# Layer 0: `v` of three groups in four by a 1x1 product and nine taps, two of them on ScalarE; two sums on GpSimd; a new order on all engines

## The chip, the cores and the metric

The kernel runs on one core of one Trainium2 chip. The metric is the device time of one execution in microseconds; the time before is the median of three runs. TensorE is called PE in the rows, VectorE DVE, ScalarE ACT and GpSimd POOL.

## The reference

Two layers, each added to its input, on four images of 64 channels and 256 x 256 pixels. Only layer 0 is touched by the change.

```python
# layer 0, x normalized by _gn first
hidden = jnp.einsum('bchw,oc->bohw', x, w_hidden) + b_hidden[None, :, None, None]
hidden = jax.lax.conv_general_dilated(hidden, w_dw[:, None, :, :], window_strides=(1, 1), padding='SAME', feature_group_count=hid, ...) + b_dw[None, :, None, None]
q, k, v = jnp.split(hidden, 3, axis=1)
out = jnp.fft.irfft2(rfft2(patches(q)) * rfft2(patches(k)), s=(8, 8))      # by 8x8 patch
out = (out - mu) / jnp.sqrt(var + 1e-05) * ln_w + ln_b                     # over the 128 channels
y = x + jnp.einsum('bchw,oc->bohw', v * out, w_proj) + b_proj
```

## The kernel before

Layer 0 works on strips of 8 image rows (128 strips in all, 32 per image) and cuts each strip into 4 groups of 64 columns, so 512 groups. A loop iteration does two strips; a "half" below is one strip, four groups, and the groups of a half are called j to j+3. Every engine has its own queue, written out by hand as a function `body`, and the engines meet at semaphores only. An engine works strictly in its order, so a wait at the head of a queue holds all that stands behind it.

What happens to a strip first: ScalarE normalizes it into `xn` (`normed`, L782, two halves), VectorE multiplies its edge rows (`masks`, L901), ScalarE rounds it to 16 bits (`high_parts`, L788), GpSimd makes the rests (`low_parts`, L573, two halves), and VectorE copies high and low parts into the stacks that TensorE reads: `high_below` (L921), `high_stacks` (two products at L910, four copies at L914 to L917) and `both_stacks` (three copies at L927). TensorE may begin a strip only when its stacks are there.

What happens to a group: `q` and `k` come out of TensorE as four tiles of 14 matmuls (`conv`, L625). ScalarE copies them (L795), TensorE makes the transform (`forward`, L697), ScalarE copies its parts (`k_swap`, `q_im`, `q_re`, L818 to L823), VectorE and GpSimd multiply and add them (`product`, L936 on VectorE; `imaginary` with its two steps L583 and L586 on GpSimd; the mean by `means`, L965 and L967, on VectorE and `less_mean`, L592, on GpSimd), and TensorE transforms back (`inverse`, L688).

`v` is made in two ways, by turns. In every second group TensorE does all of it: 14 matmuls of 512 columns (`conv_v`, L644), and ScalarE copies the result (`v_copy`, L803). In the others TensorE makes a small 1x1 product with the hidden weights (`hidden`, L660 to L664) into PSUM, and the 3x3 filter is done by taps: ScalarE does the middle one (`middle_tap`, L810), VectorE the other eight, each a multiply-add into `v_s` (`taps`, L959).

At the end of a pair of groups come `times_v` (L947, VectorE), `variance` (L714), `project` (L674 and L676), the root on ScalarE (L835, L837), and on VectorE `finish` (L982 makes `t_n`, L983 adds bias and residual) and `output` (L993 adds `t_n`, L995 takes the statistics). In part of the iterations VectorE also takes statistics of the following images (`x_chunk`, L1002).

## Time and profile before

| | us |
|---|---|
| median of three runs | 8745.06 (8741.76 to 8749.92) |
| profiled execution, its own time | 8754.59 |
| its span | 8752.8 |
| layer 0, from about 140 to 6196 us of the span | 6056 |
| busy in the whole span: TensorE, VectorE, ScalarE, GpSimd | 96%, 85%, 72%, 55% |

The granted clock of TensorE is 0.993 of its full speed as a mean over the span. The busy shares are means over both layers; what a change in layer 0 does must be read from the stretch of layer 0, and there from the order in which the four queues meet.

### The profile page before, as it was taken

The page shows a single profiled execution, that of the slowest core. Times are in us where ns is not written, and L with a number is a line of the kernel's source. Part 1 is how long each engine was busy: PE and PEld are TensorE (multiplying, and loading weights), DVE is VectorE, ACT ScalarE, POOL GpSimd, SP SyncE. Part 2 cuts the span into 40 slices and gives each one's busy share as a digit, 9 for nine tenths or more (in the row PEclk, how much of TensorE's full clock was granted, in tenths as well). Part 3 has the DMA queues.
Part 4 walks back from the last instruction along what each step waited for, and adds up shares of the span by engine and source line. Part 5 has one row for each costly group of instructions (what it writes and reads, how often), then busy time and mean ns, then how long its engine had stood idle before and what let it go on. Part 6 is the DMA issues. An engine that isn't in the chain of part 4 may idle for free. (4 is left out here: it accounts for less than half of the span.)

```text
span 8752.8 us, 169999 instructions
## 1 busy us (share of the span) xinstructions
PE 8435.8 (96%) x57716; PEld 4818.6 (55%) x57716; DVE 7480.2 (85%) x9839; ACT 6324.6 (72%) x8629; POOL 4840.4 (55%) x2723
## 2 busy tenths in 40 slices
PE   2999999999999999999999999999879999999999
PEld 1666666666666666666666666666323333333333
DVE  6888888888888888888888888888759999999998
ACT  2777777777777777777777777777208888888887
POOL 1444444444444444444444444444109999999998
PEclk9999999999999999999999999999999999999999
DMA  6222222222222222222222212212694555555554
GB/s 154 54 68 61 55 68 63 55 67 54 64 68 53 64 56 66 64 56 65 64 49 55 54 43 54 54 43 54 146 203 114 119 119 119 119 119 119 119 119 111
DMA packets 613650, 711.27 MB, mean 81 GB/s; under 512 B 44029, under 2 KB 572507, under 8 KB 589575
## 3 DMA queue, kind: packets, MB, share of 16 engines
q1 hardware_dynamic: 611022, 690.44, 33.9%
q10 hardware_dynamic: 2488, 18.98, 1.0%
q8 instruction: 87, 1.43, 0.1%
q14 instruction: 53, 0.43, 0.0%
HBM read 548.96 MB, written 164.11 MB: 81 GB/s over the span
## 5 line engine op out<-in xcount | busy, mean ns | idle before, releaser
L625 PE MATMUL banks<-w_hi,hi_lo 128*128 128x256 f16 x18432 | 2362.6, 273 | 35.1 <-DVE hi_lo L927 35.1
L625 PEld LDWEIGHTS banks<-w_hi,hi_lo 128*128 128x128 f16 x18432 | 1737.7, 98 | 844.9 <-issue 533.5
L583 POOL TENSOR_TENSOR u_im<-q_im,k_swap 128x512 f32<-128x512 f32 x512 | 741.3, 1448 | 1810.4 <-ACT q_im L821 1723.8
L959 DVE SCALAR_TENSOR_TENSOR v_s<-banks,tap_w,v_s 128x512 f32<-128x512 f32 x2048 | 1535.1, 750 | 55.0 <-ACT v_s L810 0.6
L1511 PE MATMUL banks<-z,conv_w 128*128 128x512 f32 x3096 | 1556.0, 618 | 1.2 <-ACT z L1639 1.2
L1482 POOL TENSOR_TENSOR part_sum<-part_sum,prod 128x1024 f32<-128x1024 f32 x645 | 1525.2, 2365 | 52.2
L795 ACT ACTIVATE qk<-banks,inv_wscale 128x512 f32<-128x512 f32 x1024 | 706.5, 690 | 910.2 <-PE banks L625 903.7
L586 POOL TENSOR_TENSOR u<-u,u_im 128x512 f32<-128x512 f32 x512 | 725.3, 1417 | 766.8 <-DVE u L936 766.8
L625 PE MATMUL banks<-w_lo_pair,hi_pair 128*128 128x256 f16 x6144 | 1006.1, 273 | 0.0
L592 POOL TENSOR_TENSOR u<-u,u_mean 128x512 f32<-128x512 f32 x512 | 532.2, 1040 | 733.7 <-DVE u_mean L967 733.7
L1511 PEld LDWEIGHTS banks<-z,conv_w 128*128 128x128 f32 x3096 | 521.5, 188 | 628.1 <-issue 570.5
L936 DVE TENSOR_TENSOR u<-q_re,banks 128x512 f32<-128x512 f32 x512 | 350.6, 685 | 529.9 <-ACT q_re L823 526.4
L573 POOL TENSOR_TENSOR hl_all<-xn,hi_all 64x1280 f16<-64x1280 f32 x258 | 702.1, 2721 | 137.8 <-ACT hi_all L788 100.9
L782 ACT ACTIVATE xn<-xr,par 128x1408 f32<-128x1408 f32 x258 | 746.9, 2895 | 16.7 <-DMA xr<-in_x_dram 9.8
L688 PEld LDWEIGHTS banks<-idft,u 128*128 128x128 f32 x4096 | 498.1, 192 | 261.4 <-issue 168.9
L625 PEld LDWEIGHTS banks<-w_lo_pair,hi_pair 128*128 128x128 f16 x6144 | 601.5, 98 | 69.9
L688 PE MATMUL banks<-idft,u 128*128 128x128 f32 x4096 | 568.5, 282 | 33.6 <-POOL u L592 25.0
L644 PE MATMUL banks<-hi_lo,w_hi 128*128 128x512 f16 x2304 | 544.2, 382 | 22.0 <-DVE tmp L1028 22.0
L625 PE MATMUL banks<-w_lo_one,hi_side 128*128 128x256 f16 x2048 | 558.5, 273 | 0.0
L625 PE MATMUL banks<-w_lo_one,hi_ind 128*128 128x256 f16 x2048 | 558.4, 273 | 0.0
L697 PE MATMUL banks<-qk,dft 64*32 64x512 f32 x8192 | 557.6, 601 | 0.0
L1788 DVE TENSOR_TENSOR prod<-banks,x_up 128x1024 f32<-128x1024 f32 x387 | 471.0, 1221 | 58.1 <-PE banks L1493 52.1
(252 smaller groups left out, 15777.1 us busy)
## 6 DMA issues: line engine op xcount, KB each, us to landing
xr<-in_x_dram SPq DMA_DIRECT2D x258, 640.0 KB, 9.1
xb<-y_scratch SPq DMA_DIRECT2D x262, 320.0 KB, 4.7
xa<-y_scratch SPq DMA_DIRECT2D x262, 256.0 KB, 5.4
x_res<-in_x_dram SPq DMA_DIRECT2D x258, 256.0 KB, 4.1
out_dram<-res SPq DMA_DIRECT2D x258, 256.0 KB, 3.3
y_scratch<-ys SPq DMA_DIRECT2D x256, 256.0 KB, 3.9
prod<-y_scratch SPq DMA_DIRECT2D x256, 256.0 KB, 5.6
xs<-in_x_dram SPq DMA_DIRECT2D x92, 512.0 KB, 7.4
```

What stands on the lines that cost most here:

```text
L573: nc.gpsimd.tensor_tensor(hl_all[C:P, 1 + c0:1 + c1, 1:SL], xn[C:P, c0:c1, 0:SL - 1], hi_all[C:P, 1 + c0:1 + c1, 0:SL - 1], ALU.subtract). ...
L583: nc.gpsimd.tensor_tensor(u_im[:], q_im[:], k_swap[:], ALU.mult).then_inc(u_made, 1)
L586: nc.gpsimd.tensor_tensor(u[:], u[:], u_im[:], ALU.add).then_inc(u_step, 1)
L625: r = pe.matmul(out, px, w, start=n == 0, stop=n == 13)
L644: r = pe.matmul(b_v[:], w, px, start=n == 0, stop=n == 13)
L688: last = pe.matmul(by_patch[:, p, t], u[:, block], idft[:], start=True, stop=True)
L697: last = pe.matmul(b_f[p][fr, :], dft[px, part, :], qk[px, 2 * half:2 * half + 2, :], start=True, stop=True)
L782: act.activation(xn[:, cols, 0:SL], xr[b][:, :, cols].rearrange("p s w -> p w s"), ACT.Identity, bias=par[b][:, 1:2], scale=par[b][:, 0:1] ...
L795: act.activation(qk[:, 2 * h:2 * h + 2, :], b_qk[h][:].rearrange("p (t c) -> p t c", t=2), ACT.Copy, scale=inv_wscale[:, 0:1]).then_inc(qk ...
L959: v.scalar_tensor_tensor(v_out, hidden_v[:, 1 + dc:GCOL + 1 + dc, 1 + dr:R + 1 + dr], tap_w[:, t:t + 1], v_out, ALU.mult, ALU.add).then_in ...
L1482: nc.gpsimd.tensor_tensor(part_sum[:], prod[0][:] if n == 0 else part_sum[:], prod[n + 1][:], ALU.add)\
L1511: last = pe.matmul(b_c[h][:], conv_w[:, n, :], z[b][:, 2 * h + j:2 * h + j + 2, dc:dc + W], start=n == 0, stop=n == 5)
```

## The change

It makes `v` by `conv_v` only in the first group of each strip; the three others take the 1x1 product and taps. ScalarE now does two of the nine taps: the middle one as before (`first_tap`), and the one at the lower right (`side_tap`), which it writes to a buffer of its own, `side`. VectorE does the seven left. GpSimd adds `side` to `v_s` (`side_sum`), and it takes over the sum of `t_n` into the output (`output_sum`), which VectorE did in `output`. The bodies of all engines are written in a new order, and groups are numbered so that a body reaches back into the strips before and ahead into the next; the old `tail` functions give way to bodies before the first and behind the last iteration. `k_swap`, `q_im` and `q_re` are separate steps. The sizes of all other operations stay. The core of the diff, without the functions that only take other indices:

```diff
@@ -420,6 +421,10 @@
...
+                def side_sum(i, j):
+                    if real(i, j):
+                        pool.wait_ge(v_tapped, tapped(i, j) * 7)
+                        pool.wait_ge(v_side, tapped(i, j))
+                        nc.gpsimd.tensor_tensor(v_s[j % 4][:], v_s[j % 4][:], side[:], ALU.add).then_inc(v_summed, 1)
+                def output_sum(i, jp):
+                    if real_pair(i, jp):
+                        out = ys[jp // 2 % 2][:, :, GCOL * (jp % 2):GCOL * (jp % 2) + GCOL]
+                        pool.wait_ge(fin_read, i * 4 + (jp + 1))
+                        pool.wait_ge(t_made, i * 4 + (jp + 1))
+                        nc.gpsimd.tensor_tensor(out, out, t_n[:].rearrange("p (c r) -> p r c", r=R), ALU.add).then_inc(fin_step, 1)
...
+                    for h in range(2):
+                        j, jp, js = 4 * h, 2 * h, h
+                        imaginary(i, j)
+                        if real(i, j):
+                            pool.wait_ge(u_made, i * 8 + (j + 1))
+                        low_parts(i, js + 1, 0)
+                        complex_sum(i, j)
+                        side_sum(i, j + 1)
+                        if real(i, j + 1):
+                            pool.wait_ge(v_summed, tapped(i, j + 1))
+                        low_parts(i, js + 1, 1)
+                        less_mean(i, j)
+                        imaginary(i, j + 1)
+                        complex_sum(i, j + 1)
+                        less_mean(i, j + 1)
+                        imaginary(i, j + 2)
+                        side_sum(i, j + 2)
+                        output_sum(i, jp - 1)
+                        complex_sum(i, j + 2)
+                        less_mean(i, j + 2)
+                        imaginary(i, j + 3)
+                        complex_sum(i, j + 3)
+                        side_sum(i, j + 3)
+                        less_mean(i, j + 3)
+                        output_sum(i, jp)
...
+                            pe.wait_ge(tops_ready, i * 2 + (j // 4 + 1))
+                            pe.wait_ge(stacks_ready, i * 2 + (j // 4 + 1))
...
+                    if real(i, j):
+                        if j % 4 == 1:
+                            pe.wait_ge(v_copied, i * 2 + (j // 4 + 1))
+                        else:
+                            pe.wait_ge(v_tapped, (tapped(i, j) - 1) * 7)
+                            pe.wait_ge(v_side, tapped(i, j) - 1)
+                        need(pe, t_made, i * 4 + (projected + 1))
...
+                    for h in range(2):
+                        j, jp, js = 4 * h, 2 * h, h
+                        tile(i, j, 1)
+                        tile(i, j, 2)
+                        tile(i, j, 3)
+                        inverse(i, j - 2)
+                        project(i, jp - 2, j - 1, then_forward=j)
+                        forward(i, j)
+                        value(i, j, image if h == 0 else None)
+                        inverse(i, j - 1)
+                        hidden(i, j + 1, jp - 2)
+                        tile(i, j + 1, 0)
+                        tile(i, j + 1, 1)
+                        tile(i, j + 1, 2)
+                        tile(i, j + 1, 3)
+                        variance(i, jp - 1, then_forward=j + 1)
+                        forward(i, j + 1)
+                        project(i, jp - 1, j + 1)
+                        tile(i, j + 2, 0)
+                        hidden(i, j + 2, jp - 1)
+                        tile(i, j + 2, 1)
+                        tile(i, j + 2, 2)
+                        inverse(i, j)
+                        tile(i, j + 2, 3)
+                        tile(i, j + 3, 0, then_forward=j + 2)
+                        forward(i, j + 2)
+                        tile(i, j + 3, 1)
+                        tile(i, j + 3, 2)
+                        inverse(i, j + 1)
+                        tile(i, j + 3, 3)
+                        hidden(i, j + 3, jp - 1)
+                        variance(i, jp)
+                        tile(i, j + 4, 0, then_forward=j + 3)
+                        forward(i, j + 3)
...
+                def side_tap(i, j):
+                    if real(i, j):
+                        act.wait_ge(v_hidden, tapped(i, j))
+                        need(act, v_summed, tapped(i, j) - 1)
+                        act.activation(by_column(side[:]), hidden_v[:, 2:GCOL + 2, 2:R + 2], ACT.Copy, scale=tap_w[:, 8:9])\
+                            .then_inc(v_side, 1)
...
+                        exp_root(i, jp - 2)
+                        key_swap(i, j)
+                        v_copy(i, j)
+                        query_imaginary(i, j)
+                        first_tap(i, j + 1)
+                        side_tap(i, j + 1)
+                        square(i, j - 1)
+                        high_parts(i, js + 1)
...
-                                               v_out, ALU.mult, ALU.add).then_inc(v_tapped, 1)
-
...
+                            if n == 0:
+                                v.wait_ge(v_begun, tapped(i, j))
+                                v.wait_ge(v_side, tapped(i, j))
...
+                        both_stacks(i, js)
+                        times_v(i, j - 3)
+                        product(i, j - 2)
+                        taps(i, j - 1, 0, 1)
+                        params(i, js + 2)
+                        taps(i, j - 1, 1, 3)
+                        sums(i, j - 2)
+                        taps(i, j - 1, 3, 4)
+                        means(i, j - 2)
+                        taps(i, j - 1, 4, 7)
+                        product(i, j - 1)
+                        if h == 0 and not first and (stats or image == NI - 1):
+                            x_chunk(i)
...
+                        sums(i, j - 1)
...
+                        shifted(i, jp - 2)
+                        means(i, j - 1)
+                        times_v(i, j - 2)
+                        masks(i, js + 1)
...
+                        scaled(i, jp - 2)
+                        output(i, jp - 3)
+                        product(i, j)
+                        output(i, jp - 2)
+                        taps(i, j + 1, 0, 4)
+                        times_v(i, j - 1)
+                        taps(i, j + 1, 4, 7)
+                        high_below(i, js + 1)
+                        sums(i, j)
+                        means(i, j)
+                        scaled(i, jp - 1)
+                        high_stacks(i, js + 1)
+                        taps(i, j + 2, 0, 1)
+                        product(i, j + 1)
+                        taps(i, j + 2, 1, 3)
+                        sums(i, j + 1)
+                        taps(i, j + 2, 3, 4)
+                        means(i, j + 1)
+                        taps(i, j + 2, 4, 5)
+                        times_v(i, j)
+                        taps(i, j + 2, 5, 6)
+                        shifted(i, jp - 1)
+                        taps(i, j + 2, 6, 7)
 
```

On VectorE, in an ordinary iteration, the row of stack copies at the end of a strip's preparation, before: the `high_stacks` rows, `params`, then `both_stacks` follow one another directly.

```order
L910 TENSOR_SCALAR hi_ind1<-ind,par1 64x256 x2
L914 COPY hi_pair1<-hi_all 128x2064
L915 COPY hi_ind1<-hi_all 64x2064
L916 COPY hi_side1<-hi_all 64x2064
L917 COPY hi_side1<-hi_all 64x2048
L893 COPY par0<-tab0 128x6
L927 COPY hi_lo1_0<-hl_all 128x2064
L927 COPY hi_lo1_1<-hl_all 128x2064
L927 COPY hi_lo1_2<-hl_all 128x2064
L936 TENSOR_TENSOR u<-q_re,banks1 128x512
L947 TENSOR_TENSOR w_v1<-banks3,v_s1 128x512
```

The same place now: the `both_stacks` copies (L1085) stand at the end of the half, directly behind the last tap (L1122) of group j+2.

```order
L1122 SCALAR_TENSOR_TENSOR v_s2<-banks2,tap_w,v_s2 128x512
L1135 TENSOR_SCALAR u_mean<-u_mean 128x4
L1122 SCALAR_TENSOR_TENSOR v_s2<-banks2,tap_w,v_s2 128x512
L1106 TENSOR_TENSOR w_v0<-banks3,v_s0 128x512
L1122 SCALAR_TENSOR_TENSOR v_s2<-banks2,tap_w,v_s2 128x512
L1153 SCALAR_TENSOR_TENSOR ys1<-banks3,b_proj,x_res1 128x8x64
L1122 SCALAR_TENSOR_TENSOR v_s2<-banks2,tap_w,v_s2 128x512
L1085 COPY hi_lo1_0<-hl_all 128x2064
L1085 COPY hi_lo1_1<-hl_all 128x2064
L1085 COPY hi_lo1_2<-hl_all 128x2064
```

So the copies moved behind seven taps, a product and the sums of a later group.

On GpSimd, the end of an ordinary half before: between two `less_mean` rows (L592) there is only the pair of L583 and L586.

```order
L573 TENSOR_TENSOR hl_all<-xn,hi_all 64x128x10
L583 TENSOR_TENSOR u_im<-q_im,k_swap 128x512
L586 TENSOR_TENSOR u<-u,u_im 128x512
L592 TENSOR_TENSOR u<-u,u_mean 128x512
L583 TENSOR_TENSOR u_im<-q_im,k_swap 128x512
```

And now, from the second `low_parts` row (L600) of a half on:

```order
L600 TENSOR_TENSOR hl_all<-xn,hi_all 64x128x10
L625 TENSOR_TENSOR u<-u,u_mean 128x512
L611 TENSOR_TENSOR u_im<-q_im,k_swap 128x512
L618 TENSOR_TENSOR u<-u,u_im 128x512
L625 TENSOR_TENSOR u<-u,u_mean 128x512
L611 TENSOR_TENSOR u_im<-q_im,k_swap 128x512
L633 TENSOR_TENSOR v_s2<-v_s2,side 128x512
L641 TENSOR_TENSOR ys1<-ys1,t_n 128x8x64
L618 TENSOR_TENSOR u<-u,u_im 128x512
```

The rows L633 (`side_sum`, waits for the last tap of j+2) and L641 (`output_sum`) are new on this queue and stand between L611 and L618 of group j+2.

## Rows read from the trace of the kernel before

**Rows 1.** Stretches, layer 0: start:end length, busy (x) PE, PEld, DVE, ACT, POOL, clock, DMA, GB/s.
```profile
140.00:6196.00 6056.00, 5979.95 (x50171) 4013.79 (x50172) 5122.06 (x7279) 4494.30 (x6021) 2700.99 (x1794) 1.00 0.25 59
```

**Rows 2.** One line's instructions, `v_copy`: count, shortest/median/longest ns, first to last start.
```profile
L803 ACT ACTIVATE v_s<-banks,inv_wscale x64: 662/687/694, 4605.7 to 6079.8; 128x512 f32<-128x512 f32 x64
```

**Rows 3.** Waits of TensorE, 300 to 6160 us: us in total, times, longest.
```profile
PE banks L688 <- POOL u L592: 19.4, 63, 1.6
```

**Rows 4.** Timeline of TensorE: start us, us, engine, line, operation, operands, count.
```profile
5046.65 2.11 PE L644 MATMUL banks<-hi_lo,w_hi 128*128 128x512 f16 x9
...
5049.77 1.09 PE L697 MATMUL banks<-qk,dft 64*32 64x512 f32 x16
5050.79 1.16 PE L625 MATMUL banks<-w_hi,hi_lo 128*128 128x256 f16 x9
...
5052.33 1.06 PE L688 MATMUL banks<-idft,u 128*128 128x128 f32 x8
5053.22 1.15 PE L625 MATMUL banks<-w_hi,hi_lo 128*128 128x256 f16 x9
...
5054.75 0.28 PE L660 MATMUL banks<-hi_lo,hid_hi 128*128 128x264 f16 x1
...
5055.55 1.16 PE L625 MATMUL banks<-w_hi,hi_lo 128*128 128x256 f16 x9
...
5066.82 1.08 PE L674 MATMUL banks<-v_s,proj_shift 128*64 128x512 f32 x4
...
5068.69 1.16 PE L625 MATMUL banks<-w_hi,hi_lo 128*128 128x256 f16 x9
```

**Rows 5.** One line's instructions, `both_stacks`, over the steady stretch (columns as in rows 2).
```profile
L927 DVE COPY hi_lo<-hl_all x372: 689/824/833, 339.3 to 6133.9; 128x2064 f16<-128x2064 f16 x186
```

**Rows 6.** Timeline of VectorE (columns as in rows 4).
```profile
5043.61 0.95 DVE L921 COPY hl_all<-hi_all 64x2816 f16<-64x2816 f16 x1
...
5047.91 3.81 DVE L910 TENSOR_SCALAR hi_ind<-ind,par 64x256 f16<-64x256 f16 x2
...
5053.22 0.82 DVE L916 COPY hi_side<-hi_all 64x2064 f16<-64x2064 f16 x1
5054.05 1.67 DVE L917 COPY hi_side<-hi_all 64x2048 f16<-64x2048 f16 x1
...
5055.81 2.17 DVE L927 COPY hi_lo<-hl_all 128x2064 f16<-128x2064 f16 x3
5057.90 0.68 DVE L936 TENSOR_TENSOR u<-q_re,banks 128x512 f32<-128x512 f32 x1
...
5061.35 4.68 DVE L959 SCALAR_TENSOR_TENSOR v_s<-banks,tap_w,v_s 128x512 f32<-128x512 f32 x6
5065.95 1.08 DVE L993 TENSOR_TENSOR ys<-ys,t_n 128x512 f32<-128x512 f32 x1
```

**Rows 7.** Timeline of GpSimd (columns as in rows 4).
```profile
5043.84 1.85 POOL L586 TENSOR_TENSOR u<-u,u_im 128x512 f32<-128x512 f32 x1 [0.77 <-DVE u L936]
5046.70 1.04 POOL L592 TENSOR_TENSOR u<-u,u_mean 128x512 f32<-128x512 f32 x1 [1.00 <-DVE u_mean L967]
5047.81 2.71 POOL L573 TENSOR_TENSOR hl_all<-xn,hi_all 64x1280 f16<-64x1280 f32 x1
5053.50 1.67 POOL L583 TENSOR_TENSOR u_im<-q_im,k_swap 128x512 f32<-128x512 f32 x1 [2.97 <-ACT q_im L821]
5058.73 1.28 POOL L586 TENSOR_TENSOR u<-u,u_im 128x512 f32<-128x512 f32 x1 [3.56 <-DVE u L936]
```

**Rows 8.** Timeline of ScalarE (columns as in rows 4).
```profile
5050.96 0.58 ACT L818 COPY k_swap<-banks 64x512 f32<-64x512 f32 x1 [0.40 <-PE banks L697]
...
5052.74 0.68 ACT L821 ACTIVATE q_im<-banks,imag_sign 64x512 f32<-64x512 f32 x1
...
5056.01 0.78 ACT L810 ACTIVATE v_s<-banks,tap_w 128x512 f32<-128x512 f32 x1
```

**Rows 9.** Timeline of VectorE where the next images' statistics are made.
```profile
3035.61 2.46 DVE L1002 BATCH_NORM_STATS2 x_stats<-xs 128x6 f32<-128x512 f32 x4
```

710 lines of the change are left out of this document (355 added, 355 removed).

## The prediction

> **What bounds the kernel now.** I read the stretches first: in layer 0 TensorE is busy 5980 of 6056 us, VectorE 5122, ScalarE 4494, GpSimd 2701 [rows 1]. Then the pace: 63 intervals of two groups between 4605.7 and 6079.8, 23.40 us each, so a half (one strip) takes 46.8 us [rows 2]; the halves with statistics keep this pace too. Then the waits of TensorE: only 19.4 us in 63 waits, for the mean-free product [rows 3]. So TensorE bounds layer 0 by its own work, and VectorE, with 5122 of 6056, has some 7 us of a half to spare. The last view is the timeline of all engines side by side, where VectorE and GpSimd turn out to be less independent than the busy times say.
>
> **TensorE's part.** One of the two `conv_v` of a half becomes a `hidden`. Start to start, `conv_v` takes 5049.77 - 5046.65 = 3.12 us and `hidden` 5055.55 - 5054.75 = 0.80 [rows 4]. That frees 2.32 us per half, and with 128 halves 297 us. If TensorE still bounded, the pace would be 44.5 us and the kernel 8745 - 297 = 8448.
>
> **VectorE's part.** Taps: 3 x 7 instead of 2 x 8, five more. Six taps behind one another take 4.68 with 0.75 for the last, so 0.79 from tap to tap, and the next other instruction starts 0.67 behind the last tap's start, an overlap of 0.08 [rows 6]; with it `product` and `times_v` (0.68) count 0.60. Five more taps are 3.8 us. Two sums L993 of 1.08 leave, 2.2. Net +1.6 per half: busy time alone would still fit into 44.5. On ScalarE three `side_tap` of about 0.78 and one `first_tap` for one `v_copy` of 0.69 come in [rows 8, 2], +2.4, into some 12 us of slack per half: free as long as its order keeps pace. GpSimd gets 3 `side_sum` and 2 `output_sum`.
>
> **How VectorE and GpSimd get in each other's way.** At 5047.81 GpSimd starts the 2.71 us of `low_parts`; VectorE starts its two products of `high_stacks` at 5047.91 and is through with both only at 5051.72, 1.20 after GpSimd's end at 5050.52 [rows 6, 7]. Later the copy L916 is running (5053.22 to 5054.04) when GpSimd starts L583 at 5053.50: GpSimd needs 1.67, ending 1.13 after the copy, and the next copy L917, 0.69 by itself (1.67 with 0.98 of standing), ends 0.55 after GpSimd. So these copies and GpSimd's instructions take turns, one whole instruction each, while taps (PSUM and one buffer) show no such spread. The Trainium skill, SBUF — State Buffer, section Who interferes with whom, says the same, that whoever issues first holds the shared port pair for the whole instruction and the other fully blocks; were it a mere slowing of both, the terms below would be smaller. The three copies of `both_stacks`, 2.17 us together, never met GpSimd before: their longest is 833 ns in 372 [rows 5], as GpSimd stands idle there (5055.17 to 5058.73).
>
> Now both new GpSimd instructions meet them. `side_sum` of j+2 waits for the last tap of j+2, and the instruction behind this tap on VectorE is the first copy of `both_stacks`; `output_sum` stands directly behind `side_sum`. So copy, sum (1.13), copy, sum (1.13), copy: 2.17 becomes 4.4. Behind these copies waits TensorE, which opens the next strip with a tile that needs `stacks_ready`. What `output_sum` takes on GpSimd no row shows. Bounds: 1.04 (L592, in place) and 2.71 (L573) [rows 7]; I take 1.27 as for the sums of the same size. The Trainium skill, GPSIMD Engine Reference, section Engine selection, speaks against the move: elementwise work on two inputs runs about 2x slower there than on VectorE, by which 1.08 becomes an estimated 2.2 us.
>
> **The cycle that this makes**, worked along one half. Time zero: `side_tap` of j+1 is written and VectorE starts the taps of j+1.
> - Seven taps with a `times_v` between: 3 x 0.79 + 0.67 + 0.60 + 2 x 0.79 + 0.67 = 5.9.
> - `high_below` 0.95, then a wait: the complex sum of j on GpSimd may only follow `low_parts`, and is held by `high_below` to 1.13 behind it (as 5043.84 + 1.85 against 5043.61 + 0.95), so 1.2 more. 8.0.
> - `sums`, `means`, `scaled`: 1.4. 9.4.
> - `high_stacks`. GpSimd's second `low_parts`, released by the last tap of j+1, has just started: 2.7 standing, 1.2 for the two products, `less_mean` of j between them 0.9, 3.0 for the four copies, `imaginary` of j+1 between them 0.98. 8.8 (before, without `less_mean` between: 5055.72 - 5047.91 = 7.8 [rows 6]). 18.2.
> - Seven taps of j+2, six of them followed by something else, 6 x 0.67 + 0.79 = 4.8; between them `product` 0.60, `times_v` 0.60, `shifted` 0.8 (a multiply-add like a tap), `sums` and `means` 0.8. 7.6. 25.8.
> - `both_stacks` 4.4. 30.2.
> - TensorE from the tile of the new strip to the end of `forward` j: four tiles at 1.54 = 6.2, two `forward` at 1.02, `inverse` 0.89, `project` 1.87 [rows 4]: 11.0. 41.2.
> - ScalarE then, in its order: `query_real`, `exp_root`, `key_swap`, `v_copy`, `query_imaginary`, `first_tap`, `side_tap`. Two copies at about 1.1 each, 0.6, 0.69, 1.4, 0.7, 0.7 [rows 8]: 6.6, in which TensorE makes `conv_v`, `inverse` and `hidden` beside it. 47.8, and the taps of the next strip start.
>
> So the cycle is 47.8 us against 46.8. TensorE, with 44.5 of work, then waits at three places: at `forward` j+2 for `product` j+1 (1.6), at `inverse` j+1, and above all at the first tile of a strip (2 us). Its granted clock was 1.00 through layer 0 [rows 1]; I leave it there, though waits of this length are new.
>
> In the halves with `x_chunk`, 2.46 us [rows 9], the order is `product`, `x_chunk`, `sums`, `shifted`, `means`, `times_v`, `masks`, `scaled`, and `hidden` j+1 waits for `scaled`; about 1.6 of the 2.46 lie in time that VectorE has there, 0.85 come through to the cycle, in some 46 halves: 39 us.
>
> Image changes (three), filling and draining I take as unchanged: the same chains, in other places. I take the transfers as hidden as before; the load of a strip is now asked for later, behind a later `output`, and if it came late `normed` on ScalarE would wait for it. The sum against the profiled execution: 8754.6 + 128 x 1.0 + 39 = 8922; it stood 9.5 above the median, so 8910.
>
> **The rivals.**
> 1. The copies of `both_stacks` are not met, or the sums slip behind them. The cycle is then 47.8 - 2.2 = 45.6: 8745 - 128 x 1.2 + 39 = 8630. For it: 2.2 us hang on two instructions arriving within a microsecond. Against it: both are released by the tap that stands just before the copies. 0.22.
> 2. TensorE bounds on. Both collisions would have to cost under a microsecond together: 8448, between 8400 and 8550. For it: VectorE's part of this cycle would be 23.4 us without any standing, not 30.2. Against it: 3.6 us of standing per half (2.6 and 0.98) are in the rows of before already. 0.13.
> 3. Slower still: `output_sum` takes 2.2 us. Then `both_stacks` ends 0.9 later, and `output` in front of the taps of j+1, which waits for the other `output_sum`, passes 0.4 on. 1.3 x 128 = 166: 9075. It decides from about 1.7 us on. 0.10.
> 4. Gain and loss cancel within 0.2% (17 us, about what a measurement of this kernel can tell from no change): 0.06.
>
> **How the numbers follow.** My forecast, 8910 with 8800 to 9000 of its own, gets 0.49. It is above 8762 throughout, as is rival 3: slower 0.59. Rivals 1 and 2: faster 0.34, as a sliver of rival 1 falls into no change: 0.07 with rival 4. The range takes in rival 1 and most of rival 3, and leaves out rival 2: 8590 to 9080.
>
> **What would show it.** In the new profile the copies of `both_stacks` should have a median near 1.6 us or a longest near 1.8 where it was 833 ns, `side_sum` near 1.9 to 2.0, TensorE should wait some 2 us at each strip's first tile for L1085, and two `v_copy` (now one per half) should stand 47.8 us apart. If the copies are still at 0.8, rival 1 holds; if TensorE hardly waits and the pace is 44.5, rival 2; if `output_sum` is above 2 us, rival 3. I would be wrong altogether if the hold between the two engines were weaker for 16-bit copies next to float sums than L917 shows.

## The result and the profile after

| | time, us | ratio to before, 95% interval |
|---|---|---|
| before | 8747.5 (4 runs) | |
| after | 9282.6 (9274.1 to 9285.3, 4 runs) | 1.061 (1.0591 to 1.0628) |
| predicted | 8910 (8590 to 9080) | 1.019 |

The changed kernel is 6.1% slower. Its profiled execution has a span of 9283.5 us and a mean granted clock of 0.969 (before: 8752.8 and 0.993). The direction was forecast, the size was not: the profiled execution took 9285.3 us, 363 more than the sum of 8922 that was made for it, and the median lies outside the range. Of the 531 us between the two spans 525 lie in the 127 halves of layer 0 (6505.6 us from the first `v_copy` of layer 0 to that of its last strip, against 5980.5 before); filling and draining are as long as they were, to 5 us.

The page and the stretches of the four long loops of layer 0 (columns as in [rows 1]); TensorE is no longer busy throughout, and its clock, 1.00 in [rows 1], is 0.96 to 0.97:

```profile
PE 8473.3 (91%) x57204; PEld 4892.6 (53%) x57204; DVE 7966.9 (86%) x10207; ACT 6569.2 (71%) x9010; POOL 5826.4 (63%) x3361
...
320.00:1490.00 1170.00, 1072.75 (x8831) 727.24 (x8830) 1001.98 (x1361) 840.59 (x1135) 658.07 (x432) 0.96 0.25 58
1600.00:3060.00 1460.00, 1335.54 (x10985) 905.72 (x10983) 1251.59 (x1718) 1051.81 (x1419) 816.77 (x539) 0.96 0.24 57
3160.00:4640.00 1480.00, 1355.67 (x11192) 921.47 (x11191) 1274.40 (x1741) 1066.18 (x1441) 832.38 (x547) 0.96 0.25 58
4750.00:6200.00 1450.00, 1337.38 (x11104) 910.91 (x11102) 1236.56 (x1680) 1058.73 (x1430) 820.58 (x543) 0.97 0.21 49
```

The waits of the changed kernel, 300 to 6600 us (us in total, times, longest). [rows 3] had 19.4 us in all for TensorE's wait on the mean-free product. Three kinds are new: TensorE for `both_stacks` (L1085), TensorE for nothing that the profile shows ("issue"), and VectorE for TensorE's `inverse` (L794). The remaining row, VectorE for the complex sum, has grown from 107 us:

```profile
DVE u L1095 <- PE banks L794: 439.4, 123, 7.2
DVE u_mean L1129 <- POOL u L618: 255.7, 200, 1.5
PE banks L681 <- DVE hi_lo L1085: 231.0, 109, 2.2
PE banks L681 <- issue: 166.6, 78, 3.5
```

The copies of `both_stacks`, which answer to [rows 5] (ns, shortest/median/longest), and the two new kinds of sums on GpSimd, `output_sum` (L641) and `side_sum` (L633):

```profile
L1085 DVE COPY hi_lo<-hl_all x345: 820/1772/2152, 300.3 to 6153.2; 128x2064 f16<-128x2064 f16 x173
L641 POOL TENSOR_TENSOR ys<-ys,t_n x256: 1515/1535/1979, 221.8 to 6733.4; 128x512 f32<-128x512 f32 x128
L633 POOL TENSOR_TENSOR v_s<-v_s,side x384: 1259/1280/1991, 185.4 to 6720.0; 128x512 f32<-128x512 f32 x192
```

**How long a half is.** The starts of two `v_copy`, one per half now, stand apart by different amounts. Between 5100 and 5303 us they are 48.4, 54.4, 48.4 and 51.9 us. Over the kernel the 46 halves with an `x_chunk` in them have a mean of 52.6 and the 81 others of 50.4. The shortest in the loops, 48.4, is near the 47.8 of the prediction; the others are not. (The difference of 2.2 us is not the price of `x_chunk`: it stands in the same half of an iteration as the turn of TensorE's loop, which is read below.)

One such short half on VectorE, from the first taps of j+1 to the same point in the next half:

```profile
5103.17 3.11 DVE L1122 SCALAR_TENSOR_TENSOR v_s<-banks,tap_w,v_s 128x512 f32<-128x512 f32 x4
...
5109.03 0.96 DVE L1074 COPY hl_all<-hi_all 64x2816 f16<-64x2816 f16 x1
5111.15 0.69 DVE L1129 TENSOR_REDUCE u_mean<-u 128x4 f32<-128x512 f32 x1 [1.17 <-POOL u L618]
...
5113.50 3.64 DVE L1061 TENSOR_SCALAR hi_ind<-ind,par 64x256 f16<-64x256 f16 x2
...
5118.65 1.89 DVE L1067 COPY hi_side<-hi_all 64x2064 f16<-64x2064 f16 x1
...
5121.28 0.75 DVE L1122 SCALAR_TENSOR_TENSOR v_s<-banks,tap_w,v_s 128x512 f32<-128x512 f32 x1
...
5128.71 4.58 DVE L1085 COPY hi_lo<-hl_all 128x2064 f16<-128x2064 f16 x3
5133.21 0.68 DVE L1106 TENSOR_TENSOR w_v<-banks,v_s 128x512 f32<-128x512 f32 x1
...
5151.54 1.54 DVE L1122 SCALAR_TENSOR_TENSOR v_s<-banks,tap_w,v_s 128x512 f32<-128x512 f32 x2
```

From taps to the end of the stacks this is 30.0 us (5103.17 to 5133.21), and to the next taps 18.3 more.

And TensorE's first tile of a strip, in a short half (first three rows), in the one of 51.9 us (the next four) and in the one of 54.4 us (the last two, the second and third tile of the strip):

```profile
5133.53 1.15 PE L681 MATMUL banks<-w_hi,hi_lo 128*128 128x256 f16 x9 [2.12 <-DVE hi_lo L1085]
...
5135.16 1.09 PE L815 MATMUL banks<-qk,dft 64*32 64x512 f32 x16
5136.18 1.16 PE L681 MATMUL banks<-w_hi,hi_lo 128*128 128x256 f16 x9
...
5284.65 1.19 PE L681 MATMUL banks<-w_hi,hi_lo 128*128 128x256 f16 x9 [2.12 <-DVE hi_lo L1085]
5285.64 0.84 PE L681 MATMUL banks<-w_lo_pair,hi_pair 128*128 128x256 f16 x3
...
5286.84 1.96 PE L815 MATMUL banks<-qk,dft 64*32 64x512 f32 x16
5290.80 1.14 PE L681 MATMUL banks<-w_hi,hi_lo 128*128 128x256 f16 x9 [2.01 <-issue]
...
5187.80 2.08 PE L681 MATMUL banks<-w_hi,hi_lo 128*128 128x256 f16 x9 [2.07 <-issue]
...
5190.74 2.13 PE L681 MATMUL banks<-w_hi,hi_lo 128*128 128x256 f16 x9
```

The reader is to see three things here that the first three rows don't have. In the 51.9 us half the three matmuls on `hi_pair` take 0.84 us (0.49 in a short half) and the forward transform 1.96 instead of 1.09: behind the wait the array runs at the lower of its two levels (1.2 instead of 2.4 GHz; the granted clock is 0.50 from 5285.7 to 5288.7, and 1.00 at the same place of the short half, behind a wait of the same 2.12 us). Before the second tile of the strip TensorE idles 2.01 us with no releaser. That tile is the first work of the loop's body: it is where TensorE's loop turns back. And in the 54.4 us half the clock is at 0.50 behind this turn too, from 5187.8 to 5193.4, so that nine matmuls take 2.08 and 2.13 us instead of 1.15. That is the difference between 51.9 and 54.4.

### The profile page after: what moved, and what is told of

It reads as the page before. It is cut to its first block and busy times, and to the rows that moved or that the text cites. A ratio compares the mean times of both kernels' runs of the same rounds, so it can differ in the third digit from the quotient of the medians.

```text
span 9283.5 us, 176870 instructions
## 1 busy us (share of the span) xinstructions
PE 8473.3 (91%) x57204; PEld 4892.6 (53%) x57204; DVE 7966.9 (86%) x10207; ACT 6569.2 (71%) x9010; POOL 5826.4 (63%) x3361
## 5 line engine op out<-in xcount | busy, mean ns | idle before, releaser
L681 PE MATMUL banks<-w_hi,hi_lo 128*128 128x256 f16 x18432 | 2443.9, 279 | 427.1 <-DVE hi_lo L1085 269.4
L681 PEld LDWEIGHTS banks<-w_hi,hi_lo 128*128 128x128 f16 x18432 | 1795.3, 100 | 1127.8 <-issue 900.0
L1122 DVE SCALAR_TENSOR_TENSOR v_s<-banks,tap_w,v_s 128x512 f32<-128x512 f32 x2688 | 2009.2, 747 | 58.6 <-ACT side L927 7.1
L1647 POOL TENSOR_TENSOR part_sum<-part_sum,prod 128x1024 f32<-128x1024 f32 x645 | 1525.1, 2365 | 52.5 <-POOL part_sum L1647 0.4
L618 POOL TENSOR_TENSOR u<-u,u_im 128x512 f32<-128x512 f32 x512 | 745.8, 1457 | 707.9 <-DVE u L1095 697.8
L611 POOL TENSOR_TENSOR u_im<-q_im,k_swap 128x512 f32<-128x512 f32 x512 | 694.9, 1357 | 739.3 <-ACT k_swap L936 405.8
L600 POOL TENSOR_TENSOR hl_all<-xn,hi_all 64x1280 f16<-64x1280 f32 x256 | 695.4, 2716 | 485.1 <-ACT hi_all L897 424.0
L943 ACT ACTIVATE q_im<-banks,imag_sign 64x512 f32<-64x512 f32 x512 | 351.0, 685 | 582.2 <-PE banks L815 579.0
L641 POOL TENSOR_TENSOR ys<-ys,t_n 128x512 f32<-128x512 f32 x256 | 446.4, 1744 | 305.2 <-DVE t_n L1143 296.2
L633 POOL TENSOR_TENSOR v_s<-v_s,side 128x512 f32<-128x512 f32 x384 | 555.6, 1447 | 104.5 <-DVE v_s L1122 104.5
L815 PE MATMUL banks<-qk,dft 64*32 64x512 f32 x8192 | 603.0, 648 | 1.6 <-ACT qk L904 1.6
L919 ACT ACTIVATE v_s<-banks,tap_w 128x512 f32<-128x512 f32 x384 | 297.8, 775 | 408.3 <-PE banks L757 406.1
L1085 DVE COPY hi_lo<-hl_all 128x2064 f16<-128x2064 f16 x384 | 582.1, 1571 | 0.0
```

Source lines behind the costliest of these rows:

```text
L600: nc.gpsimd.tensor_tensor(hl_all[C:P, 1 + c0:1 + c1, 1:SL], xn[C:P, c0:c1, 0:SL - 1], hi_all[C:P, 1 + c0:1 + c1, 0:SL - 1], ALU.subtract). ...
L611: nc.gpsimd.tensor_tensor(u_im[:], q_im[:], k_swap[:], ALU.mult).then_inc(u_made, 1)
L618: nc.gpsimd.tensor_tensor(u[:], u[:], u_im[:], ALU.add).then_inc(u_step, 1)
L681: r = pe.matmul(out, px, w, start=n == 0, stop=n == 13)
L815: last = pe.matmul(b_f[p][fr, :], dft[px, part, :], qk[px, 2 * half:2 * half + 2, :], start=True, stop=True)
L1085: last = v.tensor_copy(hi_lo[b][d][:], hl_all[:, :, 1 + d:1 + d + R])
```

## The experiments

The runs ask, in this order: what the turn of TensorE's loop costs (e1), what the lower clock costs (e2, e16), why a turn costs at all (e8, e17, e18), what the two sums on GpSimd cost at `both_stacks` (e3 to e7), and which part of the change brings the loss (e9 to e15).

All ratios are to the kernel before, run beside it on the same chip. "Half" is the distance of two `v_copy` in the loops.

| kernel | us | ratio, 95% interval | halves, us |
|---|---|---|---|
| after | 9282.6 | 1.061 (1.059 to 1.063) | 48.4 to 54.4 |
| e1 turn elsewhere | 9040.3 | 1.034 (1.032 to 1.035) | 48.4, and 49.0 to 50.6 |
| e2 extra tile in the wait | 8995.1 | 1.029 (1.027 to 1.030) | 48.2, 48.8; one copy to 52.9 |
| e3 output sum later | 9035.4 | 1.033 (1.031 to 1.034) | 46.9 to 47.6, and 51.4 to 53.3 |
| e4 both sums narrow | 8854.3 | 1.013 (1.011 to 1.014) | 46.0 to 46.7, and 48.6 to 50.8 |
| e5 = e1, e2, e3 | 8930.5 | 1.020 (1.018 to 1.022) | 47.8, 48.3, some 49.5 to 51.5 |
| e6 stacks early, e1 | 8808.5 | 1.006 (1.004 to 1.008) | 47.2, 47.8 |
| e7 output sum on VectorE | 9159.3 | 1.047 (1.045 to 1.049) | 48.1, 48.9, and 51 to 54 |
| e8 before, turned as after | 8795.4 | 1.0045 (1.003 to 1.006) | |
| e9 side tap on VectorE | 8730.1 | 0.9976 (0.9966 to 0.9985) | 46.4, 47.2; in the first loop some of 52 to 53 |
| e10 both on VectorE | 8625.8 | 0.986 (0.984 to 0.988) | 45.5 to 46.4; in the first loop two of 49 and 52 |
| e11 = e10, e1 | 8614.3 | 0.985 (0.983 to 0.986) | 45.5 to 46.4 |
| e12 = e11, stacks early | 8799.2 | 1.0055 (1.004 to 1.007) | 47.0, 47.9 |
| e13 side sum later | 9292.8 | 1.062 (1.060 to 1.063) | 48.3 to 55.1 |
| e14 side sum on VectorE | 9197.8 | 1.051 (1.049 to 1.052) | 48.5, 49.3, and 51 to 54 |
| e15 = e13, e1 | 9099.9 | 1.040 (1.038 to 1.041) | 48.6, 50.2, 50.9 |
| e16 = e1, extra tile before the turn | 9032.9 | 1.032 (1.030 to 1.034) | 48.2 to 48.8, and 49.4 to 52.6 |
| e17 = e16, code shifted | 8989.4 | 1.027 (1.025 to 1.028) | 48.2 to 48.8, and 49.1 to 51.6 |
| e18 = e8, code shifted | 8756.1 | 1.0003 (0.999 to 1.001) | |

### e1: where TensorE's loop turns

The last tile and transform of a half's order become the first of the next:

```diff
                         j, jp, js = 4 * h, 2 * h, h
+                        tile(i, j, 0, then_forward=j - 1)
+                        forward(i, j - 1)
                         tile(i, j, 1)
...
                         variance(i, jp)
-                        tile(i, j + 4, 0, then_forward=j + 3)
-                        forward(i, j + 3)
```

> TensorE's loop body begins one tile earlier: the first tile of a strip and the forward transform behind it are written at the head of the next half instead of at the end of this one. The order of all instructions is the same, only the point at which TensorE's loop turns back moves from behind the forward transform to before the wait for the stacks. Theory of the loop's end (in the changed kernel TensorE sits idle 2.0 to 3.0 us before the second tile of every second strip, with no releaser, exactly where its loop turns back; a clean half takes 48.4 us, one with the loop's end 51.9): the turn now falls into the wait of about 2.1 us for both_stacks, so some 2 to 3.5 us come back every two halves: 64 x 2 to 3.5 = 130 to 220 us, 9060 to 9150 us. Rival, the idle time belongs to something else that stands there (the forward transform's result, the tile's buffer), or another chain is as late: 9270 to 9290 us and the same idle time at the same instruction.

Measured: 9040, 242 us less, a little more than the upper end of the expectation. No half above 50.6 us is left in the loops. The stretch 4750 to 6200 us had 37.1 us of idle time of TensorE without a releaser in the changed kernel, and has 10.0 here, all of it in the first 150 us, at the change of image; the wait for the stacks is as long as it was (after, then this run; columns as in the waits above):

```profile
PE banks L681 <- DVE hi_lo L1085: 50.8, 24, 2.1
PE banks L681 <- issue: 37.1, 19, 3.5
```

```profile
PE banks L681 <- DVE hi_lo L1085: 57.4, 27, 2.2
PE banks L681 <- issue: 10.0, 7, 2.0
```

So the turn of the loop costs the changed kernel 240 us, and the rival (something else stands there) is out, since not one instruction changed its place in the order. But the turn's own idle time is only about half of that: from 300 to 6200 us TensorE's idle time without a releaser goes from 155.0 to 38.7 us, by 116. The granted clock rises in the same run, from 0.96 to 0.97 in the four stretches of the changed kernel to 0.98 to 0.99. Behind 31 of the 47 turns of the changed kernel it stands at the lower level, as at 5187.8 us. The other half of the 240 us is, by this, the lower clock that the turn brings; no run parts the two.

### e2, e16: the clock

```diff
                         if j % 4 == 0 and t == 0:
+                            if not isinstance(i, int) or i * 8 + j > 0:
+                                pe.wait_ge(qk_copied, i * 16 + (2 * j - 1))
+                                conv((j // 4 + 1) % 2, b_qk[0][:, 0:KQ], 12, None)
                             pe.wait_ge(tops_ready, i * 2 + (j // 4 + 1))
```

> Before TensorE waits for the stacks of a new strip it computes one tile (14 matmuls, about 1.54 us) of the old strip into the bank that the first tile of the new one then overwrites: extra work without use, laid into a wait of 2.1 us. Theory of the clock (behind that wait the granted clock is at the lower of its two levels for some tiles, the forward transform behind it takes 1.96 us instead of 1.09 in many halves): the wait left is 0.6 us, the transforms are at 1.09, the mean granted clock of layer 0 goes from 0.965 towards 1.00, and 1 to 2 us come back in about half to all of the halves: 9280 - 100 to 200 = 9080 to 9180 us. Rival, the lower clock there has nothing to do with the wait: same clock, and the extra work costs nothing or makes it slower: 9280 to 9400 us.

Measured: 8995, 287 us less, more than either theory had: extra work makes the kernel faster. The granted clock is 0.99 to 1.00 in all four stretches. But not all of the gain is the clock. In three of the four loops the turn no longer costs anything either (halves of 48.2 and 48.8), and in the second, 1600 to 3060 us, it does (52.5). To part the two, e16 has the loop turning as in e1 and puts the extra tile ahead of the turn:

```diff
                         variance(i, jp)
+                        old_tile(i, j + 4)
```

(`old_tile` is the same two lines as above.)

> The changed kernel with TensorE's loop turning before the wait for the stacks, and one tile of extra work without use (the old strip's data into the bank that the new strip's first tile overwrites) at the end of the old strip, ahead of the turn. Against the run with the turn alone (9040 us, halves of 48.4 and 50.0 to 50.5 us by turns, the longer ones with a forward transform of 1.96 us behind the wait) it measures the clock alone. Theory of the clock: all halves at 48.2 to 48.8 us, the transforms at 1.09 us, 9040 - 63 x 1.9 = 8920 us, 8890 to 8960. Rival, the longer halves have another cause: 9020 us or more.

Measured: 9033, the same as e1 and in the range of the rival, but not for the rival's reason. The stretches of e16:

```profile
320.00:1490.00 1170.00, 1108.82 (x9447) 767.84 (x9445) 1036.71 (x1408) 869.74 (x1173) 678.22 (x446) 1.00 0.25 61
...
3160.00:4640.00 1480.00, 1431.97 (x12240) 993.88 (x12239) 1342.36 (x1825) 1127.54 (x1523) 879.81 (x580) 1.00 0.25 60
```

The clock is at 1.00, but the turn is back: in the first, second and fourth loop every second half is 49.5 to 52.6 us long, with up to 2.3 us of idle time at the turn. In the third the turn is free, and there the halves are 48.4 and 48.8 where e1 had 48.4 and 50.6. That is the clock alone: 49.5 - 48.6 = 0.9 us a half. In the fourth stretch e1 has a mean of 48.9, and runs without either cost 48.3 (e2, e17): 0.6. Over 128 halves the clock is 80 to 115 us, on top of what it takes behind the turn. As a check: 242 + 80 to 115, less the quarter or so of the turn's cost that stays in the second loop, is near the 287 of e2.

### e8, e17, e18: why a turn costs, and where

> The kernel before, with one edit: TensorE's loop turns back behind the first tile and the forward transform of the next strip, where the loop of the changed kernel turns, instead of before that tile. The order of all instructions is the same. It asks whether the turn costs time by its place alone. If the turn idles TensorE 2 to 3 us wherever nothing else covers it: 64 x 2 to 3 = 130 to 190 us slower, 8880 to 8940 us, with idle time before the inverse transform that follows. If it costs time only where TensorE has just waited and has nothing queued: within 10 us of the kernel before, 8745 to 8760 us.

The edit is that of e1 the other way round, in the kernel before:

```diff
+                    if not last:
+                        pe.wait_ge(stacks_ready, i * 2 + 3)
+                        pe.wait_ge(hi_made, i * 2 + 3)
+                        pe.wait_ge(qk_copied, i * 16 + 15)
+                        conv(0, b_qk[0][:, 0:KQ], 4 * ORDER[0], lambda: transform_ready(i, 7, True))
+                        forward()
```

(and the same lines skipped at the head of the body.) Measured: 8795, 41 us above the kernel before that ran beside it, between the two expectations. The profile says why: 32.8 us of idle time in 11 waits, all of them in the first of the four loops, none in the other three.

```profile
PE banks L688 <- issue: 32.8, 11, 3.3
```

The program holds a copy of the loop for each stretch between two images' statistics, and they run the same instructions. What differs is where the copy lies in TensorE's program. e17 and e18 move all copies by 70 matmuls:

```diff
+                        if isinstance(i, int) and i * 8 + j == 0 and t == 0:
+                            for extra in range(5):
+                                conv(0, b_qk[0][:, 0:KQ], 0, None)
```

> The run with the turn before the wait and the extra tile ahead of it, with 70 matmuls (five tiles without use, 7.7 us once) added in TensorE's program ahead of all its loops. Nothing else changes but the place of the loops' code. The program has four copies of the loop, one for each stretch between two images' statistics; without the shift the turn cost 2.3 us in the first, second and fourth copy and nothing in the third. If the cost of a turn hangs on where the copy of the loop lies in the program, other copies are hit now, and the time is between 8880 (none hit) and 9080 us (all four); if it hangs on the timing of the engines alone, the same copies are hit and the time is 9033 + 8 us.

> The kernel before with TensorE's loop turned behind the first tile and forward transform (8795 us; 11 waits of 3 us, all in the first of the four copies of the loop), with the same 70 matmuls ahead of all loops. If the place of the copy decides: the waits are in another copy, in more or in none, 8755 (none) to 8950 us; if it is only the timing (the first stretch is the one in which x_chunk starts): the first copy again, 8795 + 8 us.

Measured: e18 8756, the time of the kernel before (8753), no turn waited for in any copy. e17 8989, 44 us less than e16 though it has 7.7 us more to do, and other copies are hit. The idle time of TensorE without a releaser in e17, in the four stretches 320 to 1490, 1580 to 3080, 3160 to 4640 and 4750 to 6200 us:

```profile
PE banks L681 <- issue: 25.6, 23, 2.1
```
```profile
PE banks L681 <- issue: 9.9, 21, 1.2
```
```profile
PE banks L681 <- issue: 20.6, 28, 1.6
```
```profile
PE banks L681 <- issue: 8.6, 19, 1.0
```

In e16 these were 27.8, 34.7, 9.7 and 26.5 us: the third copy was free, now the second and the fourth are. (The 9 us that remain in a free copy are 0.35 us in each iteration between the extra tile and the stacks, and some 4 us at the change of image.) So the place of a loop's code decides whether its turn costs anything: in both kernels the shift is the only thing that lasts, and with it other copies pay, or none. That the work which TensorE still has queued decides how much of it shows fits e1 and e16, but no run tests it alone. The Trainium skill, Advanced Engine Details and Errata, section ISA Cache, gives a cache of instructions with lines of 16 KB, 256 instructions each. That a jump back can fall into a line which must be fetched again is my inference from it; no run here shows a line or a fetch. The changed kernel itself was not run with its code shifted, so how much of its 240 us is bad luck of place stays open.

### e3, e4, e7: the sums on GpSimd and both_stacks

```diff
                         side_sum(i, j + 2)
-                        output_sum(i, jp - 1)
                         complex_sum(i, j + 2)
                         less_mean(i, j + 2)
+                        output_sum(i, jp - 1)
```

> On GpSimd the first output sum of a half moves behind less_mean of j+2, so that of the two new GpSimd instructions only side_sum can meet the three both_stacks copies. Theory of the meeting (each 128x512 GpSimd sum holds the copies up by its own time of about 1.1 us): the three copies take 3.4 us instead of 4.57, TensorE waits 1.0 instead of 2.1 us for them, 1.1 us per half come back or somewhat more with the clock: 9280 - 140 = 9140, 9080 to 9180 us. Rival, the chain that ends last does not pass through both_stacks (another wait ends as late): 9260 to 9300 us although the copies are shorter.

Measured: 9035, 247 us less, beyond the expected range. One copy in three is still met (the first of the two rows below; the second is e4's), and the shortest half goes from 48.4 to 46.9, by 1.5 us. TensorE's wait for the stacks falls from 2.1 to 0.8 us. The turn costs more here, 4.5 to 6.4 us in every second half, and GpSimd's own loop shows one as well (205.0 us in 52 waits of up to 4.6 us before its first instruction, 300 to 6600 us).

```profile
L1085 DVE COPY hi_lo<-hl_all x358: 818/824/1784, 299.5 to 6179.2; 128x2064 f16<-128x2064 f16 x179
...
L1085 DVE COPY hi_lo<-hl_all x369: 820/825/1775, 339.6 to 6168.9; 128x2064 f16<-128x2064 f16 x185
```

e4 lets both sums work on 8 of 512 columns (`v_s[j % 4][:, 0:8]`, `out[:, 0:1, 0:8]`):

> Part of the computation is left out: side_sum and output_sum on GpSimd add only 8 of 512 columns; all waits and orders stay. It measures what the two new GpSimd instructions cost by their length. Theory of the meeting: the three both_stacks copies take 2.2 us instead of 4.57, TensorE hardly waits for them, the clock stays up, 2.4 to 4 us per half come back: 8780 to 8980 us. Rival, the cycle is set by the number of dependent steps on VectorE and by TensorE's loop, and not by the two sums: no more than 1 us per half, 9150 to 9280 us.

Measured: 8854, within the first theory. The shortest half is 46.0. One copy is still met, now by `imaginary`, so this isn't 2.2 but 3.2 us of stacks. The turn still idles TensorE 2.6 to 3.1 us, at places where it did not wait for the stacks at all.

e7 undoes one part of the change: `output_sum` on VectorE, behind `scaled` of one pair and behind `shifted` of the other.

```diff
+                        v.tensor_tensor(out, out, t_n[:].rearrange("p (c r) -> p r c", r=R), ALU.add).then_inc(fin_step, 1)
...
                         shifted(i, jp - 1)
+                        output_sum(i, jp - 1)
                         taps(i, j + 2, 6, 7)
```

> One part of the change undone: output_sum goes back from GpSimd to VectorE, behind scaled of the pair 2h-2 and behind shifted of the pair 2h-1. All else is as in the changed kernel. Theory of the meeting and of the cycle through VectorE: both_stacks is met by side_sum alone, 3.4 instead of 4.57 us, but the two sums of 1.08 us each stand on the same chain, one before the last tap of j+2 and one before the taps of j+1: 1 us per half slower in sum, 9283 + 0 to 250, 9400 us. Rival, the length of VectorE's order is not what ends last, and only the meeting counts: 1.1 us per half faster, 9140 us or less.

Measured: 9159, 123 us less, between the two and near the rival. On VectorE the sum takes 1.10 us (shortest 1.08), on GpSimd 1.52 at its shortest; the shortest half is 48.1.

### e5, e6, e12: edits put together

> The three earlier edits together: TensorE's loop turns before the wait for the stacks, one tile of extra work without use lies in that wait, and the first output sum on GpSimd stands behind less_mean of j+2. Theory (three separate causes: the loop's turn, the lower clock behind the wait, the meeting at both_stacks; each alone gave 240, 290 and 250 us, and the shortest halves in the runs were 48.4 us, and 46.9 with the output sum later): halves of 46.9 and, where x_chunk stands, 47.6: 127 x (50.9 - 47.2) = 470 us under the changed kernel, 8810 us, 8770 to 8860. Should the three give their gains in full one on top of the other: 9283 - 775 = 8510. Rival, GpSimd's own loop, which idled up to 4.6 us at its turn in the run with the output sum later, becomes the late one: above 8900.

e5 is e1, e2 and e3 in one. Measured: 8930, above its range and in the rival's. The extra tile now stands behind the turn and TensorE has less queued when it comes: in two of the four loops the turn costs 2 us again, and in the same two GpSimd's turn shows, up to 3.9 us. Gains of 242, 287 and 247 us alone, 776 in sum, came to 352 together.

In e6 `both_stacks` stands before the last tap, where no new sum can be released, and TensorE makes the new strip's first tile before `hidden`:

```diff
+                        tile(i, j, 0)
+                        hidden(i, j - 1, jp - 3)
+                        variance(i, jp - 2, then_forward=j - 1)
+                        forward(i, j - 1)
                         tile(i, j, 1)
...
-                        both_stacks(i, js)
...
                         shifted(i, jp - 1)
+                        both_stacks(i, js + 1)
                         taps(i, j + 2, 6, 7)
```

> TensorE's loop turns before the wait for the stacks, as in the first experiment. On VectorE both_stacks stands before the last tap of j+2 instead of behind it, so that side_sum and output_sum, which wait for that tap or stand behind one that does, can't meet it. On TensorE the first tile of the new strip stands before hidden and variance instead of behind them, since these wait for the last tap. Theory of the meeting: the three copies take 2.2 us instead of 4.57, TensorE doesn't wait for them, forward j+3 starts some 2 us earlier and the clock stays up: halves of 46.0 to 46.9, 8650 to 8800 us. Rival, hidden of j+3 now waits for the last tap, which ends only 0.7 us sooner than both_stacks did without the meeting, and the turn of the loop, which no longer lies in a wait, costs its 2 to 3 us: 8850 to 9000 us.

Measured: 8809, just above the first range. The turn and the clock cost nothing here, the halves are 47.2 and 47.8, and a new wait ends last: `hidden` of j+3 waits for the last tap, and VectorE for the first tap behind it, 2.33 us in each half:

```profile
5016.07 0.75 DVE L1122 SCALAR_TENSOR_TENSOR v_s<-banks,tap_w,v_s 128x512 f32<-128x512 f32 x1 [2.33 <-ACT v_s L919]
```

e12 is the same order with both sums on VectorE:

> As the run before it, and both_stacks stands before the last tap of j+2, with TensorE's first tile of the new strip before hidden and variance. With the sums on GpSimd this order gave halves of 47.2 us, set by hidden of j+3, which waits for the last tap, and by the first tap behind it (VectorE stood 2.3 us for it). If that chain sets the end here too: 46.5 to 47.5 us a half, 8720 to 8850 us. If with GpSimd free TensorE (44.5 us of work) or VectorE (45.4) becomes the bound: 8500 to 8650 us, faster than before.

Measured: 8799, inside the first range, halves of 47.0 and 47.9, as in e6, although GpSimd is free. VectorE again stands for the first tap (1.7 us a half; 2.3 in e6); unlike in e6, TensorE also waits 1.5 us for the stacks, so that it is the same chain in part only.

### e9, e10, e11: which part of the change costs

e9 takes the side tap back to VectorE as an eighth tap, and with it `side_tap` and `side_sum` away; e10 takes `output_sum` back too; e11 is e10 with e1's turn.

```diff
-                        side_sum(i, j + 2)
...
-                        side_tap(i, j + 1)
...
-                        taps(i, j + 1, 4, 7)
+                        taps(i, j + 1, 4, 8)
```

> The other part of the change undone: the side tap goes back to VectorE as an eighth tap, ScalarE's side_tap and GpSimd's side_sum go; output_sum stays on GpSimd. The hidden product for three groups in four and the new orders stay. Terms along the cycle of a half: two taps more on the chain, +1.5 us; side_tap of 0.6 us no longer ahead of the taps; both_stacks met by output_sum alone, 1.1 us less. Sum -0.2 us per half: if these terms are the whole story, within 100 us of the changed kernel, 9180 to 9380 us. If GpSimd's new work costs more than its meetings (its own chain being late), as the run with output_sum on VectorE suggests, which was 120 us faster where none or 1 us per half slower was expected: 9150 us or less. If VectorE's busy time is what counts (+2.3 us per half): 9400 us or more.

> Both new GpSimd sums undone: the side tap is an eighth tap on VectorE, output_sum is on VectorE too; what is left of the change is the hidden product for three groups in four and the new orders on all engines. GpSimd then has nothing that meets both_stacks, which should take 2.2 us. Theory: the cost of the change lies in the cycle of the new order with the turn of TensorE's loop in it, so that without the sums a clean half still takes 47 to 48 us and the turn still costs 3 us every second half: 9000 to 9150 us. Rival: the sums on GpSimd are the whole loss, and without them the kernel is as fast as before or faster: 8750 us or less.

> As the run before it (no side_sum, output_sum on VectorE), and TensorE's loop turns before its wait for the stacks. If the turn costs here what it did in the changed kernel (240 us) the time is that of the run before it less 150 to 250 us, 8800 to 8950 us; if the turn is uncovered where TensorE has little to wait for, as one of the earlier runs showed, it gives back less than 100 us.

Measured: 8730, 8626 and 8614. e9 is 420 us below the bound of its second branch, the one of GpSimd's new work; e10 is where its rival had it, against the theory; e11 gives back 11 us, which was its second branch. The four corners of the square:

| | output sum on GpSimd | on VectorE |
|---|---|---|
| side tap on ScalarE and GpSimd | 9283 | 9159 |
| side tap on VectorE | 8730 | 8626 |

The side tap's new path costs 533 to 553 us, the output sum's 104 to 123, and the rest of the change (the hidden product for three groups in four and the new order) gains some 120 us against the kernel before. This is the largest fact on the change itself: with both sums and the side tap on VectorE the new order is faster than the kernel before (e10 0.986, 0.984 to 0.988), and moving work off VectorE is what makes it slower. e11 is 0.985 (0.983 to 0.986): the fastest kernel here, though not apart from e10.

The terms in my expectation for e9 were wrong in two places. VectorE and GpSimd of e9 in the same part of a half as above (taps of j+1 begin at 5032.40, and `complex_sum` is GpSimd's L618):

```profile
5039.02 0.95 DVE L1067 COPY hl_all<-hi_all 64x2816 f16<-64x2816 f16 x1
5039.89 0.67 DVE L1121 TENSOR_REDUCE u_mean<-u 128x4 f32<-128x512 f32 x1
...
5043.19 1.74 DVE L1054 TENSOR_SCALAR hi_ind<-ind,par 64x256 f16<-64x256 f16 x2
...
5047.98 0.75 DVE L1114 SCALAR_TENSOR_TENSOR v_s<-banks,tap_w,v_s 128x512 f32<-128x512 f32 x1
```

```profile
5034.99 2.72 POOL L600 TENSOR_TENSOR hl_all<-xn,hi_all 64x1280 f16<-64x1280 f32 x1 [2.35 <-ACT hi_all L893]
5037.79 1.27 POOL L618 TENSOR_TENSOR u<-u,u_im 128x512 f32<-128x512 f32 x1
5039.31 3.23 POOL L600 TENSOR_TENSOR hl_all<-xn,hi_all 64x1280 f16<-64x1280 f32 x1 [0.25 <-DVE v_s L1114]
```

From the last tap of j+1 to the end of `high_stacks` e9 takes 9.0 us (5039.02 to 5047.98), the changed kernel 12.25 (5109.03 to 5121.28). In the changed kernel the rows of GpSimd are:

```profile
5106.35 2.71 POOL L600 TENSOR_TENSOR hl_all<-xn,hi_all 64x1280 f16<-64x1280 f32 x1 [3.02 <-ACT hi_all L897]
5109.15 1.97 POOL L618 TENSOR_TENSOR u<-u,u_im 128x512 f32<-128x512 f32 x1
5111.08 1.26 POOL L633 TENSOR_TENSOR v_s<-v_s,side 128x512 f32<-128x512 f32 x1
5112.42 2.71 POOL L600 TENSOR_TENSOR hl_all<-xn,hi_all 64x1280 f16<-64x1280 f32 x1
```

The first `low_parts` starts 3.2 us behind the first tap instead of 2.6 (ScalarE makes `side_tap` ahead of the cast that releases it), and VectorE's taps end 0.75 us earlier. So `high_below` meets the complex sum, which takes 1.97 instead of 1.27, `sums` waits 1.17 us for it, and the second `low_parts`, behind `side_sum`, starts 3.4 us behind the last tap instead of 0.3 and runs beside `high_stacks`. The two shorter rows of taps save 1.5 us and the meetings take 3.3. The second wrong place: the copies of `both_stacks` are met twice in e9 too (median 1728 ns), by `imaginary` and `output_sum`. Only with both sums away are they at 0.82 us (e10):

```profile
L1076 DVE COPY hi_lo<-hl_all x372: 687/823/834, 336.9 to 6008.6; 128x2064 f16<-128x2064 f16 x186
```

A short half is then 46.4 us in e9, 2.0 less than in the changed kernel, or 256 us in all. The other half of the 550 us goes with it, read from the trace and not tested by itself: TensorE waits 1.0 us for the stacks instead of 2.1, its granted clock stays at 0.99 to 1.00, and the turn is waited for in only a few halves, all in the first loop.

### e13, e14, e15: parts of the side tap's path

> The changed kernel with one move on GpSimd: side_sum of j+1 stands behind the second low_parts and less_mean of j instead of ahead of them; these then wait for the last tap of j+1 directly. In the changed kernel this low_parts starts 3.4 us after the last tap (behind complex_sum and side_sum) and meets hi_ind's two products and a copy (high_stacks 7.8 us); in the run with the side tap on VectorE it started 0.3 us after the tap, high_stacks took 4.8 us and the kernel 550 us less. Theory, the delay of low_parts by side_sum: high_stacks ends 1.3 to 2.5 us earlier, the clean half goes from 48.4 to 46 to 47 us, and the 2 us wait of TensorE for the stacks shrinks with the clock's loss behind it: 8850 to 9100 us. Rival, what the side path costs is its meetings, which only move (side_sum now runs beside high_stacks): within 60 us of the changed kernel.

> side_sum of j+1 behind low_parts and less_mean, as in the first run of this group, and TensorE's loop turning before its wait for the stacks. If the turn still costs time in the first of them, 100 to 240 us less than it; if the shorter wait has taken that cost away already, the same within 30 us.

```diff
-                        side_sum(i, j + 1)
...
                         low_parts(i, js + 1, 1)
                         less_mean(i, j)
+                        side_sum(i, j + 1)
```

Measured: e13 9293, the rival's number. From the first tap to the end of `high_stacks` it is 18.2 us as before: the second `low_parts` starts at 5009.20, 2.2 instead of 3.4 us behind the last tap, and meets `means`, which takes 2.06 us instead of 0.5, and then the `side_sum` behind it meets `high_stacks`. The meetings moved. With the turn of e1 (e15) it is 193 us less, 9100; moving the turn gave the changed kernel 242.

> The side tap's product stays on ScalarE, but its sum is made on VectorE, as an add of two 128x512 tiles behind the last tap, instead of on GpSimd. It tells GpSimd's part from ScalarE's in the 550 us that the side tap on ScalarE and GpSimd costs. VectorE has as many instructions as with eight taps (an add at about 0.6 instead of a tap at 0.75), ScalarE the three side_taps of 0.6 us more. If it is GpSimd: as the run with the side tap on VectorE, 8700 to 8800 us. If it is ScalarE's side_tap, ahead of the taps and of the casts that feed low_parts: half or more of the loss stays, 8950 us or more.

Measured: 9198. This doesn't part ScalarE from GpSimd as it was meant to: the add on VectorE, which I priced at 0.6 us, takes 1.81 and 1.75 us where it meets GpSimd's complex sum and `imaginary`, and the shortest half is 48.5. What it shows is that taking the sum off GpSimd gives back 85 of the 550 us; how much is due to `side_tap` on ScalarE and how much to the add's own meetings stays open.

## Why the prediction was wrong

**The cycle was right in length.** Its steps against the short half at 5103 us: taps and `times_v` 5.9 (predicted 5.9); `high_below` with the wait for the complex sum to 8.0 (8.0), the wait 1.17 (1.2); `sums`, `means` and `scaled` 2.35 (1.4), since `means` takes 0.50 and `scaled` waits 0.4 for `project`; `high_stacks` 7.8 (8.8); taps of j+2 7.4 (7.6); `both_stacks` 4.5 (4.4). Sum 30.0 (30.2). TensorE from the first tile to the end of `forward` j 11.3 and 0.3 ahead of it (11.0), ScalarE 6.7 (6.6; the steps listed there add up to 6.3 only). 48.4 against 47.8. Two errors of 1 us, `means` with `scaled` and `high_stacks`, cancelled in the middle, which was luck.

**both_stacks.** Met by `side_sum` and `output_sum`, as said: 4.58 for 2.17, TensorE waits 2.1 us for L1085. The forecast of a median near 1.6 and a longest near 1.8 us came out at 1.77 and 2.15. `side_sum` at the median is 1.28 and not 1.9 to 2.0; only the one that meets the copies takes 1.8. Rival 1 priced the meeting at 2.2 us of the cycle; e3 took half of it away and the short half fell by 1.5.

**output_sum.** Taken 1.27 us, it takes 1.52 alone. The page of the Trainium skill that was weighed there (GPSIMD Engine Reference, section Engine selection) gave 2.2 by twice VectorE's time. The traces don't agree: measured is 1.52 against VectorE's 1.10 (e7), 1.4 times. Rival 3, slower by that alone, is out.

**x_chunk.** Predicted 0.85 us in 46 halves. In loops where neither turn nor clock costs, two halves with one `x_chunk` take 97.2 us and two without 96.6 (e17, second and fourth loop): 0.6.

**What failed** is the step "Its granted clock was 1.00 through layer 0; I leave it there, though waits of this length are new", and a term that was not in the sum at all. The wait at the first tile of a strip was forecast, with its length; what comes behind it was not. The clock drops behind it in a part of the halves, on the very chain that sets the cycle (tile, forward transform): 80 to 115 us (e16). And the changed order lets TensorE's loop turn right behind this tile, where TensorE has just caught up with its queue: 240 us (e1), some 116 of them idle time at the turn and the rest, by the clocks of e1, the clock again. So the clock, put at nothing, is 200 to 240 us as an estimate (240 - 116 + 80 to 115), and the turn's idle time near 116. Together 320 to 355 of the 363 us. The 0.6 us of a short half are 77 more, less the 11 by which `x_chunk` was over-priced, so that some 20 to 60 us stay the other way. Part of them is in the three image changes, which I took as unchanged: the halves there stand 35 us above the pace in the kernel before, and 18 to 20 in e2 and e17. The rest is open; the costs were measured one at a time, and e5 shows that they don't simply add.

**The change's parts.** The prediction put the loss on the meeting at `both_stacks` and called the rest of GpSimd's new work nearly free. e9 shows that the side tap's path cost five times what the output sum did. The 1.2 us wait for the complex sum and the standing of `high_stacks` stood in the sum, but as if they had been there anyway ([rows 6] show `high_stacks` with 7.8 us too). They are the price of one tap less: in e9, without the move, the stretch that holds them is 3.3 us shorter. Rival 2, TensorE as the bound, was out for the change as a whole, but e10 with halves of 45.5 us comes within 1 us of it.

## What to carry to other kernels

A kernel at 99% of one engine hides what its other costs are. Here TensorE came to wait 2.1 us at one place in each half, and the clock and the turn of its loop behind that place charged 320 to 355 us, more than the 128 waits themselves (269 us); with a wait of 1.0 us (e9) little of this was left. So a forecast that adds a wait of this size to TensorE should not leave its clock where it was, and should look at what stands right behind the wait. How much it costs elsewhere is not shown: one part of it hangs on where the code lies. Where instructions of two engines hold each other up, one that is moved from one engine to the other is not removed but becomes able to meet all its neighbours; list which pairs are released by the same event before counting the time saved. And when a loop's turn costs, it costs least ahead of a wait for another engine, with the wait behind the turn: moved there it gave back 242 us (e1) and 193 (e15), and 11 where there was hardly a wait (e11).

## What was not expected of the hardware

- The turn of a loop on TensorE can idle it for 1.8 to 3.5 us, or for nothing. It depends on where the copy of the loop lies: 70 matmuls ahead of all loops moved the cost from the first, second and fourth copy to the first and third (e16, e17), and took it away altogether in the kernel before (e8: 41 us, e18: none). GpSimd's loop idled GpSimd up to 4.6 us (e3); whether the place of its code matters was not tested.
- The granted clock fell to 0.50 behind waits of TensorE of 2.1 us that come once in 48 to 54 us, and behind turns of 1.8 to 3.5 us, but not behind each of them: behind 73 of 101 such waits and 31 of 47 turns (changed kernel, 300 to 6200 us).
- 14 matmuls of useless work in a wait of 2.1 us made the kernel 3.1% faster (e2): the granted clock of the four stretches went from 0.96 to 0.97 to 0.99 to 1.00.
- A sum of two fp32 tiles of 128x512 on GpSimd takes 1.27 us on flat tiles and 1.52 where one side is read and written across rows; on VectorE 1.10 for the latter.
- On VectorE an instruction as small as `means` (128x4) takes 2.06 us instead of 0.16 when it meets `low_parts` on GpSimd (e13); an output sum of 1.10 us on VectorE takes up to 1.91 (e7).
